# Moving the low half of the attended rows to POOL, and the weight preparation to other steps, in a gated cross-attention and feed-forward kernel

## The reference, cut to what matters

```python
x = x + tanh(g_xattn) * xattn(layernorm(x), ctx, ctx, ...)   # q, k, v, softmax, attn @ v, then @ Wo.T + bo
x = x + tanh(g_ffn) * ffn(layernorm(x), ...)                 # 4-bit block-quantized weights, 16-bit activations
```

```python
s = maximum(max(abs(wb), axis=-1) / 7, 1e-12)
wq = clip(round(wb / s), -8, 7) * s
```

## Time and profile before

| | |
|---|---|
| runs | 632.62 us median of 3 (632.51 to 634.73) |
| profiled execution | 634.7 us, span of its trace 632.9 us |
| attention stage | about the first 348 us of the span |
| PE busy | 567.9 us, 90% of the span |
| DVE busy | 486.7 us, 77% |
| ACT busy | 437.5 us, 69% |
| POOL busy | 202.0 us, 32% |
| mean granted TensorE clock | 0.96 |

### The profile page before, as it was taken

How to read it: one execution, slowest core, us unless ns; L and a number is a source line. 1 busy time by engine, 2 the same in 40 slices (tenths; PEclk the granted TensorE clock), 3 DMA queues, 4 the chain that set the end, 5 groups by cost and what they waited for, 6 DMA issues and landing times. The chain is left out here.

```text
span 632.9 us, 11543 instructions
## 1 busy us (share of the span) xinstructions
PE 567.9 (90%) x4271; PEld 338.0 (53%) x4271; DVE 486.7 (77%) x797; ACT 437.5 (69%) x629; POOL 202.0 (32%) x219
## 2 busy tenths in 40 slices
PE   2679999899999999999873799999999899949997
PEld 1346666566565666665442444434444344428886
DVE  5677889999999999898644298896888799964441
ACT  2226888678787787887762244437999998869960
POOL 4622347766665777653452000000000000010000
PEclk9879999999999999999986799999999999969999
DMA  6422444445435444333231000000000000013332
GB/s 189 126 85 76 129 127 129 120 138 143 147 112 136 141 128 110 111 106 106 63 83 54 2 1 0 1 1 0 1 0 1 1 1 0 1 66 101 135 134 99
DMA packets 42951, 49.12 MB, mean 78 GB/s; under 512 B 10640, under 2 KB 30480, under 8 KB 42896
## 3 DMA queue, kind: packets, MB, share of 16 engines
q1 hardware_dynamic: 41312, 43.81, 23.8%
q0 software_dynamic: 1152, 4.19, 2.1%
q10 hardware_dynamic: 432, 0.39, 0.2%
HBM read 24.58 MB, written 8.72 MB: 53 GB/s over the span
## 5 line engine op out<-in xcount | busy, mean ns | idle before, releaser
L715 DVE TENSOR_REDUCE negm<-s_ps 128x2 f32<-128x512 f32 x256 | 163.7, 682 | 28.2 <-PE s_ps L438 27.5
L606 ACT ACTIVATE pt<-st_ps 128x512 f32<-128x512 f32 x256 | 138.7, 596 | 56.1 <-PE st_ps L453 55.0
L1011 PE MATMUL pairs<-xq,wut 128*128 128x512 f16 x576 | 126.0, 379 | 6.5 <-DVE cmax L1276 3.4
L1011 PEld LDWEIGHTS pairs<-xq,wut 128*128 128x128 f16 x576 | 55.5, 98 | 77.0 <-DVE cmax L1276 7.3
L438 PE MATMUL s_ps<-kst,qst 96*128 96x256 f16 x512 | 82.9, 280 | 10.8 <-DVE negm L715 5.6
L453 PE MATMUL st_ps<-qst,kst 97*128 97x512 f16 x256 | 77.4, 383 | 0.8 <-ACT pt L606 0.8
L420 PE MATMUL pv_ps<-pt,vt 128*32 128x256 f32 x1024 | 68.5, 385 | 1.4 <-ACT ot L557 0.7
L1383 POOL PARTITION_ALL_REDUCE vmax<-vmax x5 | 1.8, 370 | 204.7 <-DVE vmax L1231 129.8
L1011 PE MATMUL pairs<-xq,wgt 128*128 128x512 f16 x288 | 65.0, 385 | 0.4 <-DVE xq L1227 0.3
L438 PEld LDWEIGHTS s_ps<-kst,qst 96*128 96x128 f16 x512 | 46.8, 99 | 34.0 <-DVE negm L715 21.2
L826 POOL TENSOR_SCALAR xn<-xt,mv,rstd 128x256 f32<-128x256 f32 x30 | 36.5, 1223 | 64.6 <-PE misc L518 64.4
(11 more groups left out here) (164 smaller groups left out, 1026.7 us busy)
## 6 DMA issues: line engine op xcount, KB each, us to landing
qst<-qk SPq DMA_DIRECT2D x96, 64.0 KB, 2.1
kst<-qk SPq DMA_DIRECT2D x45, 128.0 KB, 3.2
xt<-in_x SPq DMA_DIRECT2D x16, 256.0 KB, 4.3
ct<-in_ctx SPq DMA_DIRECT2D x16, 256.0 KB, 3.1
recb<-rec_dram SPq DMA_DIRECT2D x16, 256.0 KB
xr<-in_x SPq DMA_DIRECT2D x16, 256.0 KB, 4.0
out<-y SPq DMA_DIRECT2D x16, 256.0 KB, 4.0
lnall<-out POOLq DMA_DIRECT2D x8, 512.0 KB, 4.3
```

Of the source, the lines that this page charges most:

```text
L606: nc.scalar.activation(pt[:, (j // 2) % 2, j % 2, kt], st_ps[u % 3][:], ACT.Exp, scale=1.0 / (WS * WS * HD ** 0.5)).then_inc(exp_done, 1)
L715: nc.vector.tensor_reduce(negm[:, b % 2, tt, lo:lo + 5:4], s_ps[tt][:], AX.X, ALU.max, negate=True).then_inc(max_done, 1)
L1011: mm = nc.tensor.matmul(ps[:, p, k, :], w[:, a, dt, f * P:(f + 1) * P], xq[:, b, c, dt, :], start=n == 0, stop=n == len(terms) - 1)
```

## The change

The kernel after differs in these places:

- `al` of batches 0 to 13 is computed by POOL, at the same step 21, in POOL's order after `normalise` of place 4 and ahead of `xb` at place 6. Batches 14 and 15 stay on DVE.
- The block maxima on DVE go from place 1 to place 5, the scales from places 1 to places 5 and 6, at the steps that `SCALES` now lists.
- All pieces of the weights come one batch (8 steps) later, and DVE's clips go from place 4 to place 5.
- The load of `w_down` goes from steps 42 to 45 to steps 48 to 51.

```diff
-    SCALES = (2, 34, 66)
+    SCALES = ((-3, 5, 13, 13), (29, 37, 45, 46), (69, 77, 85, 86))
+    PIECES = 15
...
-            b, j = divmod(g - 7, PAIRS)
+            b, j = divmod(g - PIECES, PAIRS)
...
-                if 42 <= g < 46:
-                    f, d = (g - 42) // 2, (g - 42) % 2 * (F // 2)
+                if 48 <= g < 52:
+                    f, d = (g - 48) // 2, (g - 48) % 2 * (F // 2)
...
-                if (b := batch(g, 21)) is not None:
+                if (b := batch(g, 21)) is not None and b >= NB - 2:
                     dve.wait_ge(ah_done, b + 1)
                     dve.wait_ge(o_done, b)
                     nc.vector.tensor_tensor(al[:], at[:, b % 2], ah[:], ALU.subtract).then_inc(al_done, 1)
...
-                for i, at0 in enumerate(SCALES):
-                    if at0 - 1 - g in (16, 8, 0):
-                        part_scales(i, 2 - (at0 - 1 - g) // 8)
-                    if g == at0 - 1:
+                for i, steps in enumerate(SCALES):
+                    for p in range(PARTS):
+                        if g == steps[p]:
+                            part_scales(i, p)
+                    if g == steps[PARTS]:
                         if i:
                             dve.wait_ge(blk_scaled, 2 * i)
                         block_scales(i)
-                for i, n in pieces_behind(g, 4):
+                for i, n in pieces_behind(g, 5):
...
                 if (b := batch(g, -28)) is not None and b:
                     normalise(b)
+                if (b := batch(g, 21)) is not None and b < NB - 2:
+                    pool.wait_ge(ah_done, b + 1)
+                    pool.wait_ge(o_done, b)
+                    nc.gpsimd.tensor_tensor(al[:], at[:, b % 2], ah[:], ALU.subtract).then_inc(al_done, 1)
```

## The result

The kernel after takes 679.46 us (median of 4 runs, 677.22 to 683.05), against 632.57 us before. The ratio is 1.074, with a 95% interval from 1.0702 to 1.0778. It is slower by 47 us, where 681 us was forecast.

The account below looks back on a forecast made before the run. PE was taken to set the pace, DVE close behind. The profiled 634.7 us + 32.7 stall - 4.5 relief + 20 clock gave 682.9 us, so 681 us for the median; range 655 to 695 us for 8 in 10.

Parts of the forecast that it names:

- The stall: At the projection of batches 0 to 9, PE waits 3.27 us for POOL's `al`, ten times: +32.7 us.
- The clock: On PE behind the stalls, nine of ten are followed by half clock, 2.2 us each: +20 us (0 to 33).
- DVE's relief: On DVE in the attention stage, `al` leaves and the preparation moves to place 5 and 6: -4.5 us.
- The load and the pieces: Weight pieces 8 steps later and the later load of `w_down` on SP cost nothing, 1 us at most.
- (a): Rival: the stall at the projection comes but PE's clock holds, 661 us; chance 0.22.
- (b): Rival: the stall is partly taken up by PE's slack or a faster `al`, 640 to 655 us; chance 0.07.
- (d): Rival: no change, relief on DVE and a small stall on PE cancel, 633 us; chance 0.02.
- (e): Rival: every stall costs PE the longest half-clock stretch, 5.0 us, 711 us at worst; chance 0.03.
- (c): Rival: POOL's `al` is ready when the projection is due, only DVE's relief is left, 626 us; chance 0.05.

Follow-up runs that it names:

- al_only: Kernel before with `al` of batches 0 to 13 on POOL at step 21, behind `normalise`; weights' preparation at its old steps: 677.69 us, ratio 1.0699.
- weights_only: Kernel after with `al` back on DVE for all batches, so only the preparation is moved: 628.63 us, ratio 0.9926 against the kernel before.
- filler: Kernel after with 26 extra matmuls on PE in each stall of batches 0 to 9: 656.66 us, ratio 1.0395 against the kernel before.
- filler_half: Kernel after with 13 extra matmuls on PE in each stall of batches 0 to 9: 657.27 us, ratio 1.0378 against the kernel before.
- filler_old: `al_only` with 26 extra matmuls on PE in its ten stalls, preparation at its old steps: 661.82 us, ratio 1.0443 against the kernel before.
- al_ahead_old: Kernel before with POOL's `al` at step 20, ahead of `normalise`, preparation not moved: 633.11 us, ratio 1.0000.
- al_ahead: Kernel after with POOL's `al` one step earlier, at step 20, ahead of `normalise`: 627.26 us, ratio 0.9903 against the kernel before.
- al_between: Kernel after with `al` between the two `xn` instructions of `normalise` for batches 0 to 9: 657.22 us, ratio 1.0390 against the kernel before.

## Why the prediction was right

**The stall (+32.7 us).** Right in place, number and size. The forecast was 3.27 us, ten times. A batch with the stall alone takes 3.28 us more (`al_only`), and the trace of after shows ten waits of 3.1 us. The missing 0.17 us is an overlap: without a stall the projection starts 0.17 us before the scores ahead of it end in the trace (`weights_only`), and the period counts that where the idle time doesn't. In `filler` and `filler_half` a batch costs 3.09 us. The missing 0.19 us lies between the end of `al` and the first matmul, 0.06 us in their traces against 0.26 us in `al_only`; why it is shorter behind the added matmuls was not tested. `al` took 1.15 us, as `cl` said. The Trainium skill (GPSIMD Engine Reference, section 3.1) gave 1.96 times VectorE's time; the rows give 1.15 / 0.68 = 1.7, the measured `al` agrees with them, and the rows decide. Where the stall was made shorter by a changed order, the period followed: 2.07 for 2.08 us, 0.83 for 0.87.

**The clock (+20 us).** 228.30 us less ten batches of 20.83 us is 20.0 us, as forecast. The parts differ: I had nine losses of 2.2 us, and there were ten, with a mean of 2.0 us, two errors that cancel. The ten are of two sizes: six cost 1.3 to 1.6 us, with 3.4 us at half clock, and four 2.7 to 2.9 us, with 6.8 us at half. The rows of before carried this: both lengths stand in the earlier trace rows, and at 49% of the time at half they gave my 1.7 and 3.3 us. Where a loss is smaller than that, part of the time at half lies in the wait itself, as I had assumed. The step was the least certain one, and its closeness is partly luck: `al_only`, with the same stalls, lost its clock in seven of ten. Its 224.0 us less 208.3 for ten batches with a stall, and less the 2.7 us that the preparation costs in `filler_old`, leave 13 us for the clock. The Trainium skill (TensorE: Matmul & The Clock Gate, section HAM oscillation) tells of a loop that waits for a DMA for some 3 to 5 us in every turn and loses its clock in every turn. The kernel after agrees, with ten of ten stalls of 3.28 us; `al_only`, with seven of ten, agrees in part.

**DVE's relief (-4.5 us).** The sum was right for the preparation without stalls (-4.8 us in `weights_only`) and too large with them (-2.6 to -3.0 us by `filler_old`). The two terms share about 2 us: 32.8 - 4.8 counts them with the preparation, and 30.7 - 2.7 with the stalls; the sum is the same. Two side remarks failed. I allowed up to 1 us a batch for `al` leaving DVE; `al_ahead_old` shows nothing. I had taken it from the 10.4 us that PE's weight loads waited for DVE, but the loads overlap PE's matmuls: PE itself waited for `negm` for 3.4 us in that stretch. And I wrote that the scales at place 6 would cost about what they cost at place 1 if no stall covered them. They cost nothing: 17.55 us for that batch in `weights_only`. The remark took DVE's load for even over the batch, although DVE's idle time can be read by place.

**The load and the pieces (nothing).** Right: `weights_only` has both at their new steps, and all its ten batches take 17.54 or 17.55 us.

**The sum.** The profiled execution took 681.65 us, where the sum for it was 682.9. In its trace 32.8 - 4.8 + 20.0 give the 48.0 us of the ten batches; the start and what lies behind the ten batches took off 1.3 us together (-2.5 and +1.2), for which the sum had no term.

**The rivals.** (a), no clock loss, is what `filler` makes of the kernel: 657 us where 661 was given, 2 us of it by the shorter stall. (b) and (d) did not come, and neither did (e): the dearest loss of clock in one batch was 2.9 us. (c), `al` in time, is what `al_ahead` makes of it: 627 us where 626 was given. Its condition was that POOL be through `xn` and `al` when the projection is due; the experiment has only `al` done by then, ahead of `xn`, and lost nothing, since `xn` waits for PE anyway.

The best kernel is `al_ahead`, 1.0% faster than before; `weights_only` is 0.7% faster, and their intervals overlap. Nearly all of that is the preparation. The move of `al` to POOL, alone, gives nothing.

## What to carry to other kernels

Before work goes to an engine that looks idle, ask where in its queue it will stand, and what the instruction ahead of it waits for. Here POOL's idle third was for the most part one wait for PE, and work put behind that wait was late for PE one step later. Read an engine's idle time by place in the loop, not as a share: that shows both where work can be put (DVE's places 5 and 6, right ahead of its waits at 7 and 0) and where it can't. And if the engine that stalls is PE, count its clock with the stall: 3.3 us of waiting cost 5.3 us in the mean of the kernel after.

## What the runs showed of the hardware

- PE's idle time in a busy loop can cost its clock, and more often the longer it is: 0.7 us and 1.5 us never did in ten batches each, 1.9 us did in six of ten, 3.1 us in ten of ten in the kernel after and in seven of ten in `al_only`. The length alone doesn't decide it, since waits of one length went both ways, and in the kernel before half clock followed a wait of 1.25 us with little work around it.
- The clock can fall behind the wait and not in it: 0.3 to 1.1 us after PE had begun again in all six losses of `al_between` and, at 0.7 to 1.1 us, in three of ten of the kernel after.
- Matmuls with no use keep the clock. Filling 1.4 us of each stall was enough, and 13 or 26 of them made no difference (657.3 and 656.7 us).
